# The first attention of an eight-stage kernel on 32-row groups of TensorE, with half heads as the unit

## What is computed

```python
def _L0_attn_ref(x, Wqkv, bqkv, Wo, bo):
    HEADS = 16
    B, S, D = x.shape               # 1, 2048, 128
    hd = D // H                     # 8
    qkv = x @ Wqkv.T + bqkv
    qkv = qkv.reshape(B, H, S, 3 * hd)
    q, k, v = jnp.split(qkv, 3, axis=-1)
    scores = jnp.einsum('bhsd,bhtd->bhst', q, k) * (1.0 / math.sqrt(hd))
    attn = jax.nn.softmax(scores, axis=-1)
    vals = jnp.einsum('bhst,bhtd->bhsd', attn, v)
    return vals.reshape(B, S, D) @ Wo.T + bo

x = x + _L0_attn_ref(_layernorm(x, axis=-1), ...)
```

## Time and profile before

| | us |
|---|---|
| median of 3 runs | 3474.54 (3467.3 to 3480.65) |
| span of the profiled execution | 3463.3 |
| block of the projection, with loading of the first head, to the first maximum | 19.0 to 75.5 |
| maxima of head 0 alone | 75.5 to 117.6 |
| the 512 steps of scores, to the last output | 117.6 to 953.9 |
| output projection of the stage | 953.9 to 985 |
| all other stages | 985 to 3463.3 |

### The profile page before, as it was taken

One profiled execution on the slowest core, in us unless ns is written; L12 is line 12 of the kernel. 1 busy time (PEld: TensorE's weight loads), 2 busy tenths in 40 slices (PEclk: granted clock), 3 DMA queues, 4 the chain that ended last, 5 costly groups with the idle time before them and its releaser, 6 DMA issues. The chain is left out here.

```text
span 3463.3 us, 39811 instructions
## 1 busy us (share of the span) xinstructions
PE 3092.5 (89%) x14168; PEld 1729.6 (50%) x14168; DVE 2371.1 (68%) x4742; ACT 1441.1 (42%) x2519; POOL 811.3 (23%) x623
## 2 busy tenths in 40 slices
PE   5999999999978999999999999999997575566799
PEld 3444444444354555555555555555544243444576
DVE  5877777877327777777777777777745667665553
ACT  0466666666721444444444444443442203000343
POOL 2000000000002444344444444434440000444100
PEclk6799999999986999999999999999998676555698
DMA  3011011010013111101111111111100000000100
GB/s 79 3 13 13 7 13 13 7 13 7 1 44 74 37 29 33 29 21 37 37 37 37 37 37 25 32 24 31 37 1 12 0 7 2 1 1 3 29 1 13
DMA packets 35834, 76.13 MB, mean 22 GB/s; under 512 B 5926, under 2 KB 27356, under 8 KB 28636
## 3 DMA queue, kind: packets, MB, share of 16 engines
q1 hardware_dynamic: 35636, 73.59, 10.4%
HBM read 17.74 MB, written 5.24 MB: 7 GB/s over the span
## 5 line engine op out<-in xcount | busy, mean ns | idle before, releaser
L875 ACT ACTIVATE l1a_PT<-l1a_st 128x512 f32<-128x512 f32 x1024 | 604.9, 598 | 874.8 <-PE l1a_st L784 867.8
L892 DVE TENSOR_REDUCE l1a_m<-l1a_aux 128x1 f32<-128x512 f32 x1024 | 673.4, 686 | 185.7 <-PE l1a_aux L747 170.5
L429 DVE TENSOR_REDUCE l0s_m<-l0s_mx 128x1 f32<-128x512 f32 x1024 | 634.8, 683 | 203.2 <-PE l0s_mx L351 203.2
L843 POOL TENSOR_TENSOR l1a_acc<-l1a_acc,l1a_PT 128x1024 f32<-128x1024 f32 x224 | 555.6, 2480 | 716.0 <-ACT l1a_PT L875 716.0
L414 ACT ACTIVATE l0s_PT<-l0s_st 128x512 f32<-128x512 f32 x1024 | 554.7, 601 | 325.7 <-PE l0s_st L369 320.0
L797 PE MATMUL l1a_ov<-l1a_PT,l1a_V 128*64 128x512 f32 x2048 | 510.1, 620 | 0.0
L351 PE MATMUL l0s_mx<-l0a_KS,l0a_QS 96*128 96x512 f32 x1024 | 447.2, 462 | 11.5 <-DMA l0a_KS<-qk_parts 11.5
L782 PE MATMUL l1a_st<-l1a_QA,l1a_KA 128*128 128x512 f32 x1024 | 451.2, 441 | 2.3 <-issue 2.3
L784 PE MATMUL l1a_st<-l1a_QB,l1a_KB 65*128 65x512 f32 x1024 | 413.7, 404 | 0.0
L369 PE MATMUL l0s_st<-l0a_QS,l0a_KS 97*128 97x512 f32 x1024 | 402.7, 408 | 10.9 <-ACT l0s_PT L414 8.7
L747 PE MATMUL l1a_aux<-l1a_KA,l1a_QA 128*128 128x512 f32 x1024 | 404.6, 437 | 7.1 <-DMA l1a_QA<-l1a_lo 5.5
(11 more groups left out here) (350 smaller groups left out, 3105.4 us busy)
## 6 DMA issues: line engine op xcount, KB each, us to landing
l1a_KA<-l1a_hi SPq DMA_DIRECT2D x32, 512.0 KB, 7.9
l1a_QA<-l1a_hi SPq DMA_DIRECT2D x16, 512.0 KB, 4.6
l1a_QA<-l1a_lo SPq DMA_DIRECT2D x16, 512.0 KB, 4.1
l1a_QB<-l1a_hi SPq DMA_DIRECT2D x16, 512.0 KB, 4.6
l1a_KB<-l1a_lo SPq DMA_DIRECT2D x16, 512.0 KB, 6.5
l0a_QS<-qk_parts SPq DMA_DIRECT2D x64, 64.0 KB
l0a_KS<-qk_parts SPq DMA_DIRECT2D x64, 64.0 KB
l3f_w<-in_L_ffn_w SPq DMA_DIRECT2D x3, 792.0 KB
```

Of the source, the lines that this page charges most:

```text
L429: nc.vector.tensor_reduce(m4[:, h % 2, q, c:c + 1], src, axis=AX.X, op=ALU.max).then_inc(mx_read, 1)
L843: nc.gpsimd.tensor_tensor(acc[:, h % 2, 1, :], first, PT[:, g % PT_SLOTS, :], ALU.add).then_inc(added_pool, 1)
L875: nc.scalar.activation(PT[:, g % PT_SLOTS, (u % 2) * CW:(u % 2 + 1) * CW], st[:, u % ST1, :], ACT.Exp).then_inc(exp_done, 1)
L892: nc.vector.tensor_reduce(m4[:, b, q, c:c + 1], src, axis=AX.X, op=ALU.max).then_inc(aux_read, 1)
```

## The change

The two blocks become one, `l0_attend`, with these differences.

- **Row groups.** `QS` and `KS` now hold the stack of 24 rows (q hi, q lo, q hi against k hi, k hi, k lo; the product of the two low parts is left out) at partitions 0, 32, 64 and 96. Group g of KS has only the keys 512g to 512g+511; QS has all queries in each group. Row 24 of KS is -1 and row 24 of QS is the maximum itself.
- **Half heads.** A unit is 1024 queries of a head (32 units). Each has 16 steps. A step is one maxima task (two matmuls of 24 rows in two row groups, each to a bank of its own) and two score matmuls of 25 rows, in the other two row groups.
- **Maxima.** `mx` is a ring of 2 slots of 2 banks, and DVE reduces 1024 columns at once: 512 reductions in place of 1024. It then waits for its own reduction and frees the slot by an increment that is an instruction of its own. A tensor_tensor takes the maximum of two partial maxima. With query 8k+i in place k of tile i the result needs no transposition: four DMAs a unit (L493) write 128 pieces of 8 floats each into row 24 of each group. The stationary operand of a maxima matmul is now every 8th column of QS.
- **Lead.** Scores follow the maxima by 21 steps (`LEAD0`), of which 16 are the unit.
- **Values.** V is 9 columns wide; the four matmuls still go to four column groups. `ov` is one bank; ACT copies it (at step 3 of the next unit) before the next unit's values may start. The output goes through 4 fp32 matmuls with a selecting matrix (`sel`, L313) instead of transpositions, once a unit.
- **Projection.** Its matmuls and V's use the slots of `mx`. ACT does bias, scale and rounding, DVE the remainder; parts are written for each 512 tokens, and head 0 is loaded after two of these four. V for heads 4 to 15 is made in three tasks between the first maxima, at steps 2, 4 and 6.
- **Loads.** 24 DMAs a head: 12 of 64 KB for QS, 12 of 16 KB for KS.
- The semaphores of the block are handed on, and POOL clears them in the block of `token_major_out`.

```diff
+GR0 = 4
+R0 = 3 * HD0
+TILES0 = HALF0 // P
+UNITS0 = 2 * H0
+STEPS0 = 16
+LEAD0 = STEPS0 + 5
+LAG0 = 3
+BUF0, MX0, ST0, PT0 = 3, 2, 3, 6
...
+        if g < ALL:
+            out.append(("max", g))
+        if g in (2, 4, 6):
+            out.append(("v", g // 2))
+        u, s = divmod(g - LEAD0, STEPS0)
+        if s == 7 and 1 <= u <= UNITS0:
+            out.append(("ot", u - 1))
...
+                    for e in range(2):
+                        r = slice(32 * (2 * pair + e), 32 * (2 * pair + e) + R0)
+                        q = QS[r, h % BUF0, half * HALF0:(half + 1) * HALF0].rearrange("r (k i) -> r i k", i=TILES0)
+                        last = nc.tensor.matmul(o[:, e, :], q[:, tile, :], KS[r, h % BUF0, :], start=True, stop=True)
...
+                    for j in range(TPC):
+                        last = nc.tensor.matmul(o[:, 0, 32 * j:32 * (j + 1)], osb[:, i % 2, j * P:(j + 1) * P],
+                                                sel[:, :, :], start=True, stop=True)
...
+                    r = slice(32 * (2 * pair + e), 32 * (2 * pair + e) + R0 + 1)
+                    at = half * HALF0 + qc * CW
+                    nc.tensor.matmul(st[:, b % ST0, :], KS[r, h % BUF0, a * P:(a + 1) * P], QS[r, h % BUF0, at:at + CW],
+                                     start=True, stop=True).then_inc(st_full, 1)
...
+                pe.wait_ge(exp_done, 4 * (k + 1))
                 if n == 0:
+                    if u == 0:
+                        pe.wait_ge(ov_zeroed, 1)
+                    else:
+                        pe.wait_ge(o_copied, u)
...
+            for g in range(END):
+                for key in plan[g + 1]:
+                    mx_task(key)
+                at = g - LEAD0
+                if 0 <= at < ALL:
+                    scores(at)
+                if at % 2 and LAG0 <= at < ALL + LAG0:
+                    values((at - LAG0) // 2)
...
+                u, s = divmod(g, STEPS0)
+                if s == 3 and u >= 1:
+                    copy_out(u - 1)
...
+                    nc.vector.tensor_reduce(mpair[:, u % 2, tile, pair:pair + 1],
+                                            mx[:, n % MX0, :, :].rearrange("p e k -> p (e k)"),
+                                            axis=AX.X, op=ALU.max).then_inc(reduced, 1)
+                    dve.wait_ge(reduced, i + 1)
+                    dve.sem_inc(mx_free[n % MX0], 1)
...
+                sp.wait_ge(m_done, u + 1)
+                for g in range(GR0):
+                    sp.dma_start(QS[32 * g + R0:32 * g + R0 + 1, h % BUF0, half * HALF0:(half + 1) * HALF0]
+                                 .rearrange("a (k i) -> a k i", i=TILES0).bitcast(F32),
+                                 mrow[:, u % 2, :].bitcast(F32)).then_inc(m_placed[u % 2], 16)
+                if half == 0 and u >= 2 and h + 2 < H0:
                     load(h + 2)
```

More of the change, by code:

```diff
@@ new lines, in mx_task @@
+                n = slot[key]
+                if n >= MX0:
+                    pe.wait_ge(mx_free[n % MX0], n // MX0)
+                o = mx[:, n % MX0, :, :]
+                if kind == "qk":
+                    for j in range(2):
+                        last = nc.tensor.matmul(o[:, j, :], Wt[:, j, :], xnT[:, i * CW:(i + 1) * CW],
+                                                start=True, stop=True)
+                elif kind == "v":
+                    for t in range(TPC):
+                        at = slice((TPC * i + t) * P, (TPC * i + t + 1) * P)
+                        nc.tensor.matmul(o[:, 0, t * D:(t + 1) * D], xnT[:, at], Wt[:, 2, :], start=True, stop=False)
+                        last = nc.tensor.matmul(o[:, 0, t * D:(t + 1) * D], ones[0:1, 0:P], bv[0:1, :],
+                                                start=False, stop=True)
+                elif kind == "max":
+                    u, tile, pair = max_step(i)
+                    h, half = divmod(u, 2)
+                    if i % (2 * STEPS0) == 0:
+                        pe.wait_ge(heads_in[h % BUF0], 16 * LOADS0 * (h // BUF0 + 1))
+                    for e in range(2):
+                        r = slice(32 * (2 * pair + e), 32 * (2 * pair + e) + R0)
+                        q = QS[r, h % BUF0, half * HALF0:(half + 1) * HALF0].rearrange("r (k i) -> r i k", i=TILES0)
+                        last = nc.tensor.matmul(o[:, e, :], q[:, tile, :], KS[r, h % BUF0, :], start=True, stop=True)
@@ new lines, in values @@
+            def values(k):
+                u, n = divmod(k, QUADS0)
+                pe.wait_ge(exp_done, 4 * (k + 1))
+                if n == 0:
+                    if u == 0:
+                        pe.wait_ge(ov_zeroed, 1)
+                    else:
+                        pe.wait_ge(o_copied, u)
+                    if u % (2 * TPC) == 0:
+                        pe.wait_ge(v_done, u // (2 * TPC) + 1)
+                for g in (2 * k, 2 * k + 1):
+                    _, qc, pair, a = score_step(g)
+                    for e in range(2):
+                        col = 32 * (2 * qc + e)
+                        last = nc.tensor.matmul(ov[col:col + HD0 + 1, :], V[:, u // 2, KPG0 * (2 * pair + e) + a, :],
+                                                PT[:, g % PT0, e, :], start=(n == 0), stop=(n == QUADS0 - 1),
+                                                skip_group_check=True)
@@ L485, in _ @@
             sp.wait_ge(loaded.sem, loaded.all)
+        @block.gpsimd
+        def _(pool):
+            for handle in used:
+                nc.gpsimd.sem_clear(handle)
         @block.tensor
```

378 lines of the change are left out of this document (170 added, 208 removed).

## The result

| | before | after |
|---|---|---|
| median | 3473.2 (4 runs beside it) | 3785.6 (4 runs, 3783.8 to 3796.1) |
| span of the profiled execution | 3463.3 | 3782.0 |
| start of the last multiply into `vals` on DVE, the last output of the first attention | 954.9 | 1273.0 |
| the rest of the program | 2508 | 2509 |

The ratio is 1.091, 95% interval 1.089 to 1.093: 9.1% slower, 312 us. Forecast was 3393. The whole difference lies in the first attention, where the two profiled executions are 318 us apart. Of the rivals it is the fourth, the clock, with 3677, and even that was too low.

A forecast was written before the change was run, and what follows sets the result against it. DVE was taken as the bound at 1.35 a step; 45.5 + 781 + 16 + 28 + 2.4 = 873 against 953.9, so 81 less and a median of 3393. Forecast range 3345 to 3425 (45%); about 80% from 3310 to 3505.

The forecast's parts named there:

- rival 4: First attention: PE waits for DVE every step, clock may stay low; two steps 3.65, unit 32.9, program 3677; chance 11%.
- Against: at 1.2 GHz PE would have no gaps: Argument against a low clock in the first attention: PE without gaps, as in 118 to 124, after which it rose.
- forecast 24.6: A unit of 16 steps: DVE's 21.6, small DVE work, and stalls of copy and output task; 787 for 32.
- DVE is now the bound (1.35 against 1.02): Per step of the attention: DVE needs 1.35, PE 1.02 with row groups side by side, so DVE sets the pace.
- The reduction: One DVE reduction of 1024 columns per step takes 1.21.
- The wait and the separate increment: DVE's wait for its own reduction and separate increment add 0.14, so 1.35 a step.
- A pair side by side at one matmul's price: Maxima and scores on PE: two matmuls in different row groups cost one 0.235.
- The V tasks: Making V for 12 of 16 tiles between the first maxima: three tasks, 5.3 each, 16 in all.
- rival 3: Maxima's strided weight loads on PE: slower from 2.7 times a plain load, 3522 at 4 times; 13% with the late row.
- First maximum: Start of the stage: first maxima at 45.5 against 75.46 before, 30 saved.
- The row of maxima: Four DMAs a unit land after 5.9, within a cover ending at 6.4; costed at nothing.
- Copy and output task: Once a unit each, DVE stalls 1.2 behind the copy of `ov` and 1.05 behind the output task.

The follow-up runs named there:

- run with 33 rows: Kernel before with its padding rows left out, so matmuls have 32 and 33 rows in place of 96 and 97: 4492.3, against 3462.4 on the same chip.
- two groups of 64: Changed kernel with two row groups of 64 padded partitions in place of four of 32, copy one step earlier and output task one step later: 3441.3 (ratio 0.992).
- the version with rows, tasks and order all changed: Changed kernel with two padded 64-row groups, copy and output task moved, and values put between third and fourth score of two steps: 3380.2 (ratio 0.975).
- first run with two groups: Changed kernel with two row groups of 64 partitions, padded, in place of four of 32, copy and output task not moved: 3531.5 (ratio 1.019).

## Why the prediction was wrong, point by point

**The step that failed** is in rival 4, "Against: at 1.2 GHz PE would have no gaps, as in 118 to 124, after which it rose". It read that rise as an effect of matmuls back to back. Those matmuls had 96 and 97 rows. With 33 rows the same stream, as dense, stays at 0.50 for 1780 us. "A quarter of the rows in use" stood in the rival as an aside, and the whole rival was given 11%; it was the cause. The Trainium skill (TensorE: Matmul & The Clock Gate, Part 1) explains the higher clock by how busy TensorE is and names pauses as what loses it. The run with 33 rows, busy 1299.83 of 1300 at 0.50, goes against that for matmuls of few rows, and the measurement decides. Part 3 of the same page of the Trainium skill recommends row groups for shallow matmuls; the trace agrees that they run side by side (600.21 and 600.22) and not that the kernel gains by it.

**What the low clock and the order cost.** The last output came at 1273 in place of 873. From one row of maxima to the next it is 36.95 us (113.51 to 150.46), forecast 24.6. For 30 units that is 370 of the 400. Of the 12.35 a unit, 8 x (4.15 - 2.70) = 11.6 are the pairs of steps, 0.14 the copy (two steps with it take 5.49, so 1.34), 1.4 the output task (6.58, so 2.43 against 1.05); the 0.75 of small DVE work went under PE's time. Not all of the 11.6 is clock: at 1.00 two steps took 3.01 with two groups of 64, so by that estimate the clock is 8 x 1.14 = 9.1 of it, and the other 2.5 is the step below. The tail is 20 longer, the start 4. Rival 4 itself had the low clock and missed the size: its 3.65 for two steps leaves out 0.5, of which the waiting score is the part that the trace shows. Its other 3.7 a unit (32.9 less 8 x 3.65), for which it gives no working, was right: 36.95 less 8 x 4.15 is 3.75. With 4.15 it would have come to about 3677 + 8 x 31 x 0.5 = 3800.

**A second step failed under it.** "DVE is now the bound (1.35 against 1.02)" compared sums of work and left PE's order out. Where the clock was back, two steps took 3.01 and not 2.70, about 8 x 0.31 = 2.5 a unit or 80 us in all. In the changed order of the values they took 2.75. So even with its clock at 1.00 the kernel as written would, by this estimate, not have made 3393; the version with rows, tasks and order all changed made 3380.

**Terms that held.** The reduction: 1.224 for 1.21. The wait and the separate increment: reductions follow each other in 1.37, forecast 1.35. A pair side by side at one matmul's price: at 2.4 GHz 0.25 (503.95 to 504.20 in the first run with two groups), forecast 0.235. The V tasks: DVE waits 4.68, 4.99 and 4.68, forecast 5.3 each.

**A term left at nothing.** The strided weight loads of rival 3. At the lower clock they cost little: median 308 ns beside 283 for the plain ones. At the higher clock they do cost, as the first run with two groups shows (L309 strided, L329 plain), with the kernel before beside it, where L351 is plain:

```profile
L309 PEld LDWEIGHTS l0s_mx<-l0s_KS,l0s_QS x1024: 308/311/339, 40.9 to 975.0; 63*128 63x128 f32 x171
L329 PEld LDWEIGHTS l0s_st<-l0s_QS,l0s_KS x1024: 182/205/335, 85.2 to 1009.0; 64*128 64x128 f32 x171
```

```profile
L351 PEld LDWEIGHTS l0s_mx<-l0a_KS,l0a_QS x1024: 186/189/333, 75.5 to 903.6; 96*128 96x128 f32 x171
```

That is 0.12 more a load, about twice the 0.11 at which rival 3 priced a plain one, and under the 2.7 times from which it would have set the pace. Behind the values nothing hides it: the maxima to the next scores take 0.46 (503.49 to 503.95), where the kernel before has 0.34 (504.32 to 504.66). So about 0.12 of the 0.31 above is, by this estimate, the stride. The rule of the Trainium skill that was weighed there (Advanced Engine Details and Errata, SBUF Cachelines), that touching another line of 16 bytes with each access costs, fits these loads at the higher clock. No run here changes the stride alone.

**Terms that were off but small.** First maximum at 49.3, forecast 45.5. The row of maxima lands 2.0 after its issue in the median, 3.2 at most, forecast 5.9. The issue of the first four in the timeline, and the group of DMAs from 80 to 95 (KB each, median us to landing), in the kernel after:

```profile
86.44 2.50 SPq L493 DMA_DIRECT2D l0s_QS<-l0s_mrow  x4
```

```profile
l0s_QS<-l0s_mrow SPq DMA_DIRECT2D x4, 4.0 KB, 2.0
```

So the small pieces of a row of maxima landed sooner than the forecast took from the pace of a full load. Copy and output task together cost 3.0 a unit at the higher clock (two steps of 4.63 and 4.43 beside 3.02 in the first run with two groups), forecast 2.25.

## What to carry to other kernels

Before cutting rows from a matmul, or splitting it over row groups, ask what granted clock the new shape will get, and look for a stretch of that same shape in a trace, not for a dense stretch of another. Rows of zeros can be the cheapest thing in a kernel: here they took 553 us off one version, and taking them out of another cost 1030. When a sum of work says which engine is the bound, walk once through the order of the in-order engine; here, moving the longest group ahead of the one wait in front of it gave 61 us.

## What the runs showed of the hardware

- Matmuls of few rows kept the granted clock low however densely PE was fed: 0.50 for maxima and scores of 24 to 33 rows, single or in pairs, and for single ones of 64 and 65 but for two stretches of about 10 us, with PE busy 91 to 100%. Rows of zeros counted as rows.
- With single matmuls of 96 and 97 rows, or two of 63 and 64 side by side, the stretches of steps above had 0.86 to 1.00. In the unit shown it fell at stalls of 1.55 and 0.91, and the maxima alone, with a pause before each, stood at 0.50 with 96 rows as well.
- Not shown: what single matmuls of 66 to 95 rows get, and whether rows or groups of 32 rows count. The kernel after used all four groups with 24 and 25 rows each, and no run padded them to 32.
- Matmuls of 128 rows mixed in raised it in part: two more a step gave 0.86, one more gave nothing.
- A weight load of every 8th fp32 column took 308 to 311 ns at either clock; a plain one took 283 at the lower and about 190 to 205 at the higher.
- Values on two column groups took as long as twice as many on four, 1.03 and 1.04.
- A cast from fp32 to fp32r on DVE took 5.16, 4.46 and 4.01 beside fills on POOL, each ending 0.27 to 0.28 after a fill, and 0.43 without; the same rounding on ACT took 0.63 beside them.
